# Layer 2 attention of a four-layer kernel: two-pass scores, and row maxima carried by DMA one tile at a time

## The chip, the cores and the metric

The kernel runs on one core of a Trainium2 chip. The metric is device time in microseconds, the median of the runs. Engines: PE (matmul; PEld is its weight load), DVE (vector), ACT (scalar), POOL, and SP, which here only issues DMAs.

## What is computed

Four layers in turn on x, 4 sequences of 1024 tokens, 256 wide; after each, x = layernorm(x + layer(x)). The change lies in the second, a causal softmax attention with 8 heads of 64, whose values come from routed experts:

```python
q = (x @ w_q).reshape(b, n, HEADS, DIM_HEAD).transpose(0, 2, 1, 3)
k = (x @ w_k).reshape(b, n, HEADS, DIM_HEAD).transpose(0, 2, 1, 3)
...
values = jnp.einsum('bhne,ehdk,bnd->bhnk', gm, value_experts, x)
sim = jnp.einsum('bhid,bhjd->bhij', q * SCALE, k)
causal_mask = jnp.triu(jnp.ones((n, n), dtype=bool), 1)
sim = jnp.where(causal_mask, jnp.finfo(sim.dtype).min, sim)
attn = jax.nn.softmax(sim, axis=-1)
out = jnp.einsum('bhij,bhjk->bhik', attn, values)
```

## The kernel before

`layer2` (L429) loops over the four sequences. Each passes three stages, blocks in which every engine has its own written-out order and which end in a barrier: `gates_and_values` (L470: routing weights, values), `attention` (L590) and `output_experts`. Semaphores alone tie the engines together; nothing is scheduled by a planner.

**Precision.** A fast matmul takes operands rounded to float32r. So q and k are split into a rounded part (hi) and a rest (lo). For head h, slot h % 4 of `kst` holds k hi on one half of the 128 partitions and k lo on the other; `qst` holds q hi on both; `qlo` q lo on both. The scores of a key tile (128 keys by up to 512 queries, a "unit"; 12 units per head) are three matmuls in one PSUM bank: kst x qst (L662), kst x qlo (L663), and -max of each query, as `negones` x `shift` (L666), where `shift` is the identity times the maxima. A unit on the diagonal gets a mask matmul too (L665). Three banks (0 to 2) rotate.

**Maxima.** Before that, `maxima` (L648, L650) computes the scores of a query tile by all its keys with hi parts only, 1024 keys wide down to 128, into banks 3 and 4; DVE takes their row maxima (L769) and POOL makes `shift` (L785). For the first five tiles of a head, PE waits until the maximum before has been read; later the two banks alternate. In head 0, banks 5 and 6 are used too.

**The rest.** ACT takes exp of each unit (L703). `weighted` (L674, fp32) sums probabilities times values over key tiles in banks 5 and 6; its first one waits until DVE has copied the head before to `oT` (L759) and ACT its denominators (`den`, L725), which SP sends to `dens` (L622). `project` (L635) makes q and k of two heads in four parts (k, k, q, q, each 512 tokens), through bank 7; ACT copies the hi parts (L715, L718), DVE subtracts for the lo parts (L749, L753).

**The order.** Steps 0 to 9, each of eight k: scores of head step-2, maxima of head step-1, and in steps 0, 2, 4, 6 the projection of the next two heads at k = 0, 1, 2, 4. The last weighted sum of a head comes before the next head's first scores:

```python
for step in range(H0 + 2):
    h1, h2 = step - 1, step - 2
    for k in range(NT):
        if h2 >= 0:
            scores(h2, k)
        ...
    if h2 >= 0:
        weighted(h2, NT - 1)
```

Below, "head n's stretch" is the time from its first score matmul to the next head's, whatever else runs in it.

Of the kernel before, what the change touches and what calls it, by code (L numbers as in the profile page):

```python
# [29 lines left out]
P = 128  # L30
# [391 lines left out]
ATTN2 = ("qk_mm qk_hi qk_parts max_mm max_read shift_ready score_mm exp_ready pv_mm o_read den_read "  # L422
# [6 lines left out]
def layer2(nc, ctx, m, I, src, dst):  # L429
# [39 lines left out]

    def gates_and_values(own):  # L470
# [14 lines left out]
        with nc.Block() as block:  # L485
# [7 lines left out]
            def _(pe):  # L493
# [7 lines left out]
                for n, (h, t) in enumerate(order):  # L501
# [10 lines left out]
                    last.then_inc(s.value_mm, 1)  # L512

# [76 lines left out]
    def attention(own, b):  # L590
# [3 lines left out]
        kst, qst, qlo = (sb(n, [P, RK, T], F32R) for n in ("kst", "qst", "qlo"))  # L594
        shift = sb("shift", [P, 2, T], F32R)
        prob = sb("prob", [P, 2, T])
        mx = sb("mx", [P, H0, NT])
# [5 lines left out]
        parts = [(kind, n) for kind in "kq" for n in range(NH)]  # L603
        part_at = {0: 0, 1: 1, 2: 2, 4: 3}
# [10 lines left out]
        with nc.Block() as block:  # L615
            @block.sync
            def _(sp):
                fetch_load(sp, m, s, src[(b + 1) % SEQS])
                sp.dma_start(oe[:, :, :], I["oe2"][:, 0]).then_inc(s.oe_in, 16)
                for h in range(H0):  # L620
                    sp.wait_ge(s.den_read, h + 1)
                    sp.dma_start(dens[h:h + 1, :], den[den_row(h), h % 2, :]).then_inc((s.even_den_out, s.odd_den_out)[h % 2], 16)  # L622
                sp.wait_ge(s.even_den_out, 16 * (H0 // 2))
# [4 lines left out]
            def _(pe):  # L628
# [10 lines left out]
                def maxima(h, k):  # L639
                    t = NT - 1 - k  # L640
                    if k == 0:
                        pe.wait_ge(s.qk_parts, 4 * (h // 2 + 1))
# [10 lines left out]
                def scores(h, k):  # L653
                    for n, (kk, lo, hi) in enumerate(units, U * h):
                        if kk != k:
                            continue
                        if n % U == 0:
                            pe.wait_ge(s.shift_ready, NT * (h + 1))
                        if n >= 3:
                            pe.wait_ge(s.exp_ready, n - 2)  # L660
                        out, keys = bank(m.ps, n % 3, 0, hi - lo), kst[:, h % RK, k * P:(k + 1) * P]
# [16 lines left out]
                for step in range(H0 + 2):  # L678
                    h1, h2 = step - 1, step - 2
                    for k in range(NT):  # L680
                        if h2 >= 0:
                            scores(h2, k)
                        if step % 2 == 0 and step < H0 and k in part_at:
                            project(step // 2, part_at[k])
                        if 0 <= h1 < H0 and k < NT - 1:
                            maxima(h1, k)
                        if h2 >= 0 and k >= 1:
                            weighted(h2, k - 1)
                        if 0 <= h1 < H0 and k == NT - 2:
                            maxima(h1, NT - 1)  # L690
                    if h2 >= 0:
                        weighted(h2, NT - 1)

            @block.scalar
            def _(act):
# [10 lines left out]
                def hi_parts(c, j):  # L706
# [5 lines left out]
                    for odd in (0, 1):  # L712
                        got, slot = bank(m.ps, proj_bank(c, j), 0, HALF, half(odd)), (2 * c + odd) % RK
                        if kind == "k":
                            last = act.copy(kst[half(odd), slot, cols], got)  # L715
# [11 lines left out]
                for step in range(H0 + 2):  # L727
                    h2 = step - 2
                    for k in range(NT):
                        if h2 >= 0:  # L730
                            exps(h2, k)
                        if k == 0 and h2 >= 1:
                            den_out(h2 - 1)
                        if k == 3 and step == H0 + 1:
                            fetch_sd(act, m, s)
                        if step % 2 == 0 and step < H0 and k in part_at:
# [1162 lines left out]
```

## Time and profile before

| | us |
|---|---|
| median of 3 runs | 3823.37 (3819.16 to 3826.95) |
| the profiled execution | 3819.95 |
| its span, first to last instruction | 3818.2 |
| PE busy | 3343.3 (88%) |
| DVE, ACT, POOL busy | 2084.4, 1465.2, 830.3 |
| mean granted TensorE clock | 0.930 of full |

The profile comes from one execution, so sums are made against its own 3819.95. An engine's busy share is a mean over stages with different limits; of a busy PE one must know that matmuls overlap, so that what one matmul costs is the distance from its start to the next start. In idle columns the name behind the arrow is what ended the wait.

### The profile page before, as it was taken

How to read it: one execution, taken by the hardware profiler on the slowest of the kernel's cores; microseconds unless marked ns; L12 is line 12 of the kernel's file. 1: busy time of each engine (PE TensorE's matmuls, PEld its weight loads, DVE VectorE, ACT ScalarE, POOL GpSimd, SP SyncE). 2: the span in 40 equal slices, each digit the busy share in tenths (PEclk: the TensorE clock that was granted, in tenths of full speed). 3: DMA queues.
4: the chain of work that ended last, by engine and by line, in shares of the span. 5: the costliest groups of instructions: out<-in, count | busy, mean ns of one | idle time of the engine just before them, and what ended most of it. 6: DMA issues, size and time to landing. Idle time of an engine off the chain costs nothing. (4 is left out here: it accounts for less than half of the span.)

```text
span 3818.2 us, 51310 instructions
## 1 busy us (share of the span) xinstructions
PE 3343.3 (88%) x18610; PEld 2417.7 (63%) x18610; DVE 2084.4 (55%) x3495; ACT 1465.2 (38%) x2638; POOL 830.3 (22%) x908
## 2 busy tenths in 40 slices
PE   6896898988989989888998698998989698989898
PEld 4555655975568755786558555546465476767676
DVE  4346844677445954569446474756657433333333
ACT  2321144412444134431344355563645433434343
POOL 1111411743137422454216300101010000000000
PEclk9897999988999999989999899998998899999999
DMA  5111100110011100111002101000000310000000
GB/s 180 44 44 56 44 1 24 52 40 28 1 45 42 35 22 1 68 32 44 1 1 75 56 2 24 1 13 13 2 23 2 117 52 12 12 12 12 12 12 12
DMA packets 139735, 121.01 MB, mean 32 GB/s; under 512 B 79696, under 2 KB 121936, under 8 KB 136016
## 3 DMA queue, kind: packets, MB, share of 16 engines
q1 hardware_dynamic: 139472, 117.45, 10.1%
q8 instruction: 172, 2.82, 0.3%
q14 instruction: 91, 0.75, 0.1%
HBM read 100.23 MB, written 28.31 MB: 34 GB/s over the span
## 5 line engine op out<-in xcount | busy, mean ns | idle before, releaser
L1378 ACT ACTIVATE l3b_prob<-sums 128x512 f32<-128x512 f32 (+3 forms) x768 | 333.0, 494 | 205.1 <-PE sums L1311 166.6
L1628 PE MATMUL sums<-l4a_uhi,l_h 128*128 128x512 f32 x1024 | 405.8, 396 | 0.0
L1628 PE MATMUL sums<-l4a_ulo,l_h 128*128 128x512 f32 x1024 | 403.8, 394 | 0.0
L842 POOL TENSOR_TENSOR l2c_rlo<-l2c_routed,l2c_rhi 128x512 fp32r<-128x512 f32 x256 | 348.4, 1374 | 214.0 <-ACT l2c_rhi L868 177.9
L769 DVE TENSOR_REDUCE l2b_mx<-sums 128x1 f32<-128x1024 f32 (+7 forms) x256 | 192.0, 757 | 318.9 <-PE sums L650 318.2
L703 ACT ACTIVATE l2b_prob<-sums 128x512 f32<-128x512 f32 (+3 forms) x384 | 186.6, 491 | 397.7 <-PE sums L666 393.2
L1673 DVE TENSOR_TENSOR l4a_ulo<-l4a_made,l4a_uhi 128x512 fp32r<-128x512 f32 x192 | 132.1, 688 | 375.1 <-ACT l4a_uhi L1641 374.2
L222 POOL COPY sb_x<-sb_nx 128x2048 f32<-128x2048 f32 x12 | 23.0, 1914 | 1322.6 <-POOLq L1742 571.1
L952 PE MATMUL sums<-l2c_ohi,l2c_rhi 128*128 128x256 f32 x1024 | 294.4, 287 | 12.8 <-POOL l2c_rlo L842 12.1
L674 PE MATMUL sums<-l2b_prob,l_vx 128*128 128x512 f32 (+3 forms) x768 | 301.0, 506 | 3.3 <-ACT l2b_den L725 1.9
L1306 PE MATMUL sums<-l_qst,l_kst 64*128 64x512 f32 (+3 forms) x768 | 279.3, 427 | 16.4 <-DMA l_qst<-l3b_peak 6.7
L952 PE MATMUL sums<-l2c_ohi,l2c_rlo 128*128 128x256 f32 x1024 | 291.9, 285 | 0.0
L952 PE MATMUL sums<-l2c_olo,l2c_rhi 128*128 128x256 f32 x1024 | 291.8, 285 | 0.0
L785 POOL TENSOR_SCALAR l2b_shift<-sb_ident,l2b_mx 128x128 fp32r<-128x128 f32 x256 | 154.2, 605 | 603.7 <-DVE l2b_mx L769 491.0
L1289 PE MATMUL sums<-l_kst,l_qst 64*128 64x512 f32 (+3 forms) x768 | 244.1, 443 | 18.9 <-DVE l3b_low L1390 10.4
L905 DVE TENSOR_TENSOR l2c_routed<-l_oT,sums 128x512 f32<-128x512 f32 x256 | 171.6, 682 | 149.3 <-PE sums L942 148.2
L868 ACT CAST l2c_rhi<-l2c_routed 128x512 fp32r<-128x512 f32 x256 | 158.2, 621 | 238.2 <-DVE l2c_routed L905 236.8
L1306 PEld LDWEIGHTS sums<-l_qst,l_kst 64*128 64x128 f32 x768 | 140.8, 195 | 153.9 <-ACT l3b_prob L1378 133.6
L203 PE MATMUL sums<-sb_ident,sb_nx 128*128 128x128 f32 x256 | 61.0, 421 | 194.4 <-issue 93.0
L1628 PEld LDWEIGHTS sums<-l4a_uhi,l_h 128*128 128x128 f32 x1024 | 192.4, 188 | 47.5
L1628 PEld LDWEIGHTS sums<-l4a_ulo,l_h 128*128 128x128 f32 x1024 | 192.4, 188 | 45.6
L662 PE MATMUL sums<-l2b_qst,l2b_kst 128*128 128x512 f32 (+3 forms) x384 | 207.5, 540 | 7.9 <-POOL l2b_shift L785 7.9
(247 smaller groups left out, 8141.3 us busy)
## 6 DMA issues: line engine op xcount, KB each, us to landing
l_ve<-ve SPq DMA_DIRECT2D x34, 512.0 KB, 4.0
l_oe<-oe SPq DMA_DIRECT2D x16, 1024.0 KB, 6.2
sb_nx<-sums SPq DMA_DIRECT2D x15, 1024.0 KB, 5.5
l2c_word<-weights_copy SPq DMA_DIRECT2D x32, 352.0 KB, 4.0
weights_copy<-h SPq DMA_DIRECT2D x2, 4096.0 KB, 25.9
l_qst<-l3b_peak SPq DMA_DIRECT2D x512, 0.5 KB, 2.0
l_h<-weights_copy SPq DMA_DIRECT2D x2, 4096.0 KB, 23.9
sb_nx<-tokens SPq DMA_DIRECT2D x5, 1024.0 KB, 5.7
```

What stands on the lines that cost most here:

```text
L662: pe.matmul(out, keys, qst[:, h % RK, lo:hi], start=True, stop=False)
L674: last = pe.matmul(bank(m.ps, PV, lo, hi), vx[:, k, h, :], prob[:, k % 2, lo:hi], start=(k == 0), stop=True, skip_group_check=True)
L703: act.activation(prob[:, k % 2, lo:hi], bank(m.ps, n % 3, 0, hi - lo), ACT.Exp, scale=SCALE0).then_inc(s.exp_ready, 1)
L769: dve.reduce_max(mx[:, h1, t:t + 1], bank(m.ps, max_bank(h1, k), 0, (t + 1) * P), AX_X).then_inc(s.max_read, 1)
L842: pool.tensor_tensor(rlo[:, i % RT, :], routed[:, i % RT, :], rhi[:, i % RT, :].bitcast(F32), ALU.subtract).then_inc(s.routed_lo, 1)
L868: act.copy(rhi[:, i % RT, :], routed[:, i % RT, :]).then_inc(s.routed_hi, 1)
L905: dve.tensor_tensor(routed[:, i % RT, :], oT[:, c, n * HALF:(n + 1) * HALF], bank(m.ps, 4 + i % 4), ALU.mult).then_inc(s.routed, 1)
L952: last = pe.matmul(m.ps[:, t * D:(t + 1) * D], r[:, k % RT, cols], w[:, c % 2, e, :], start=(c == e == 0 and t % 2 == 0 and r is rhi and w ...
L1289: last = pe.matmul(bank(m.ps, at, 0, hi - lo), qst[rows(a), p, t * P:(t + 1) * P], kst[rows(a), p, lo:hi], start=True, stop=True)
L1306: last = pe.matmul(bank(m.ps, part % SCORE, 0, hi - lo), kst[rows(a), p, k * P:(k + 1) * P], qst[rows(a), p, lo:hi], start=True, stop=True)
L1378: act.activation(prob[:, i % RB, j, a, 0:hi - lo], bank(m.ps, part % SCORE, 0, hi - lo), ACT.Exp, scale=SCALE1).then_inc(s.exp_ready, 1)
L1628: run(lambda out, a, x, first, last: pe.matmul(out, a, x, start=first, stop=last))
```

## The change

- **Two passes.** `qlo`, `shift` and L663 go. New tiles `krow` and `qrow` hold, per slot, 65 rows: k hi (64 rows) over a row of -1, and q lo over a row of maxima. A unit is now kst x qst and krow x qrow, which gives k hi x q lo - max. (k lo x q lo was in the sum before and is not now.) ACT copies k hi twice; DVE makes q lo once instead of twice.
- **Maxima.** POOL's multiplication goes (it only sets the row of -1 once). `mx` is float32r, and SP sends each tile's 128 maxima, one element per partition, into row 64 of `qrow`. SP waits for each maximum in turn; the denominators of the head before are sent after the eighth.
- **Ticks.** The three loops now run over one counter x. Maxima of head h are at ticks 8 + 8h onwards, scores at 18 + 8h (two ticks later than the end of the maxima), and the weighted sum of a key tile comes in the tick after its scores, also across heads. The parts are k, k, q (second half of the tokens), q (first half), at ticks 0 to 3 and then every second tick from the first scores of heads 0, 2 and 4.
- **Warm-up matmuls** with no use of their result: 8 after the values, 8 after the first projections, 1 after each maxima of head 0.

```diff
+    def warm(pe, at, times):
+        for _ in range(times):
+            pe.matmul(bank(m.ps, at), sel[:, 0, :], sel[:, 0:HALF // P, :], start=True, stop=True)
...
                     last.then_inc(s.value_mm, 1)
+                warm(pe, 7, 8)
...
+        parts = [("k", 0), ("k", 1), ("q", 1), ("q", 0)]
+        WAIT = 2
+        APART = 2
+        ticks = NT * (H0 + 2) + WAIT + 1
+        scored_in = lambda x: divmod(x - 2 * NT - WAIT, NT)
+        peaked_in = lambda x: divmod(x - NT, NT)
...
+        def project_in(x):
+            if x < 4:
+                return 0, x
+            c, ahead = divmod(x - WAIT, 2 * NT)
+            if 1 <= c < H0 // 2 and ahead in range(0, 4 * APART, APART):
+                return c, ahead // APART
...
                 for h in range(H0):
+                    if h >= 2:
+                        sp.wait_ge(carried[h % 2], carried_to(h - 2))
+                    if h >= RK:
+                        sp.wait_ge(s.score_mm, U * (h - RK + 1))
+                    for k in range(NT):
+                        t = NT - 1 - k
+                        sp.wait_ge(s.max_read, NT * h + k + 1)
+                        sp.dma_start(qrow[DH0:ROWS, h % RK, t * P:(t + 1) * P].bitcast(F32),
+                                     mx[:, h, t:t + 1].bitcast(F32)).then_inc(carried[h % 2], 16)
+                    if h >= 1:
+                        den_row_out(h - 1)
+                den_row_out(H0 - 1)
...
-                        pe.matmul(out, keys, qst[:, h % RK, lo:hi], start=True, stop=False)
-                        pe.matmul(out, keys, qlo[:, h % RK, lo:hi], start=False, stop=False)
+                        pe.matmul(out, kst[:, h % RK, at], qst[:, h % RK, lo:hi], start=True, stop=False)
...
-                        pe.matmul(out, m.negones[:, :], shift[:, h % 2, lo:hi], start=False, stop=True).then_inc(s.score_mm, 1)
+                        pe.matmul(out, krow[0:ROWS, h % RK, at], qrow[0:ROWS, h % RK, lo:hi], start=False,
+                                  stop=True).then_inc(s.score_mm, 1)
...
+                for x in range(ticks):
+                    h2, k2 = scored_in(x)
+                    h1, k1 = peaked_in(x)
+                    if has(h2):
+                        scores(h2, k2)
+                    if project_in(x):
+                        project(*project_in(x))
+                        if x == 3:
+                            warm(pe, 6, 8)
+                    if has(h1):
+                        maxima(h1, k1)
+                        if h1 == 0:
+                            warm(pe, PROJ, 1)
+                    h2, k2 = scored_in(x - 1)
+                    if has(h2):
+                        weighted(h2, k2)
```

**PE, from head 0's last tiles into head 1.** L674 / L713 are weighted sums, L662 / L701 the first score pass, L648 / L685 maxima, L650 / L687 and L665 / L703 masks. Before:

```order
L674 MATMUL sums<-l2b_prob,l_vx 128x256 [waits l2_attn_exp_ready]
L674 MATMUL sums<-l2b_prob,l_vx 128x128 [waits l2_attn_exp_ready]
L662 MATMUL sums<-l2b_qst,l2b_kst 128x512 [waits l2_attn_exp_ready,l2_attn_shift_ready]
L663 MATMUL sums<-l2b_qlo,l2b_kst 128x512
L665 MATMUL sums<-sb_mask_kq,sb_ident 128x128
L666 MATMUL sums<-l2b_shift,sb_negones 128x512
L662 MATMUL sums<-l2b_qst,l2b_kst 128x512 [waits l2_attn_exp_ready]
L663 MATMUL sums<-l2b_qlo,l2b_kst 128x512
L666 MATMUL sums<-l2b_shift,sb_negones 128x512
L648 MATMUL sums<-l2b_kst,l2b_qst 128x512 [waits l2_attn_max_read,l2_attn_qk_parts]
```

Twelve more rows follow before the first weighted sum of head 1. In the changed kernel:

```order
L687 MATMUL sums<-sb_mask_qk,sb_ident 128x128
L713 MATMUL sums<-l2b_prob,l_vx 128x128 [waits l2_attn_exp_ready]
L701 MATMUL sums<-l2b_qst,l2b_kst 128x384 [waits l2_attn_exp_ready]
L703 MATMUL sums<-sb_mask_kq,sb_ident 128x128
L704 MATMUL sums<-l2b_qrow,l2b_krow 128x384
L701 MATMUL sums<-l2b_qst,l2b_kst 128x512 [waits l2_attn_exp_ready]
L704 MATMUL sums<-l2b_qrow,l2b_krow 128x512
L685 MATMUL sums<-l2b_kst,l2b_qst 128x512 [waits l2_attn_max_read]
L685 MATMUL sums<-l2b_kst,l2b_qst 128x128
L687 MATMUL sums<-sb_mask_qk,sb_ident 128x128
L713 MATMUL sums<-l2b_prob,l_vx 128x512 [waits l2_attn_den_read,l2_attn_o_read,l2_attn_exp_ready]
```

Between the last weighted sum of head 0 (128x128) and the first of head 1 (128x512) stood 20 matmuls with a whole first tile's scores and maxima; now 8 stand there.

**DVE, start of head 2's stretch.** L769 / L806 are the maxima, L749 / L789 the k lo parts, L759 / L798 the copy of a finished head. Before:

```order
L769 TENSOR_REDUCE l2b_mx<-sums 128x1 [waits l2_attn_max_mm] x8
L759 COPY l_oT<-sums 64x1024 [waits l2_attn_pv_mm]
L769 TENSOR_REDUCE l2b_mx<-sums 128x1 [waits l2_attn_max_mm]
L749 TENSOR_TENSOR l2b_kst<-sums,l2b_kst 64x512 [waits l2_attn_qk_hi]
L749 TENSOR_TENSOR l2b_kst<-sums,l2b_kst 64x512
L769 TENSOR_REDUCE l2b_mx<-sums 128x1 [waits l2_attn_max_mm]
```

In the changed kernel:

```order
L806 TENSOR_REDUCE l2b_mx<-sums 128x1 [waits l2_attn_max_mm] x8
L789 TENSOR_TENSOR l2b_kst<-sums,l2b_kst 64x512 [waits l2_attn_qk_hi]
L789 TENSOR_TENSOR l2b_kst<-sums,l2b_kst 64x512
L798 COPY l_oT<-sums 64x1024 [waits l2_attn_pv_mm]
L806 TENSOR_REDUCE l2b_mx<-sums 128x1 [waits l2_attn_max_mm] x2
```

The copy of the finished head has moved behind a maximum and the two subtractions, which wait for ACT.

**ACT, a k part.** Before:

```order
L715 CAST l2b_kst<-sums 64x512 [waits l2_attn_qk_mm]
L715 CAST l2b_kst<-sums 64x512
L715 CAST l2b_kst<-sums 64x512 [waits l2_attn_qk_mm]
L715 CAST l2b_kst<-sums 64x512
L718 CAST l2b_qst<-sums 64x512 [waits l2_attn_qk_mm]
```

In the changed kernel:

```order
L755 CAST l2b_kst<-sums 64x512 [waits l2_attn_qk_mm]
L756 CAST l2b_krow<-sums 64x512
L755 CAST l2b_kst<-sums 64x512
L756 CAST l2b_krow<-sums 64x512
L755 CAST l2b_kst<-sums 64x512 [waits l2_attn_qk_mm]
```

Two more copies stand in each k part.

## Rows read from the trace of the kernel before

**Rows 1.** The page, part 1: busy us, share of span, instructions.
```profile
PE 3343.3 (88%) x18610; PEld 2417.7 (63%) x18610; DVE 2084.4 (55%) x3495; ACT 1465.2 (38%) x2638; POOL 830.3 (22%) x908
```

**Rows 2.** Busy time by stretches: second attention stage, and the sum of four.
```profile
core 0: us, PE busy (x) PEld busy (x) DVE busy (x) ACT busy (x) POOL busy (x), PEclk, DMA share, GB/s
...
900.20:1107.50 207.30, 189.51 (x768) 113.21 (x768) 96.65 (x149) 84.07 (x155) 38.54 (x64) 0.94 0.03 11
...
sum 825.20, PE 754.36 PEld 451.04 DVE 386.38 ACT 335.98 POOL 154.18; mean PE 188.59 PEld 112.76 DVE 96.60 ACT 84.00 POOL 38.54
```

**Rows 3.** The same view, heads 1, 4, 5 and 7 of the second stage.
```profile
955.90:976.20 20.30, 20.30 (x89) 12.84 (x89) 7.08 (x9) 6.90 (x13) 4.84 (x8) 0.92 0.00 1
...
1023.90:1052.90 29.00, 26.22 (x107) 15.08 (x106) 15.63 (x22) 13.74 (x25) 4.79 (x8) 1.00 0.00 1
...
1052.90:1071.70 18.80, 18.80 (x89) 12.03 (x89) 7.11 (x9) 6.79 (x13) 4.85 (x8) 1.00 0.01 1
...
1090.40:1107.50 17.10, 16.15 (x70) 10.11 (x69) 8.27 (x31) 9.62 (x17) 0.00 (x0) 1.00 0.01 2
```

**Rows 4.** Timeline (start, us) of PE, then ACT: second and third stage's start.
```profile
900.30 5.98 PE L635 MATMUL sums<-l_xT,l_wk 128*128 128x512 f32 x8 [4.57 <-PEq L485]
...
916.10 1.22 PE L648 MATMUL sums<-l2b_kst,l2b_qst 128*128 128x512 f32 x2 [6.38 <-DVE l2b_qlo L753]
...
925.18 0.80 PE L662 MATMUL sums<-l2b_qst,l2b_kst 128*128 128x512 f32 x1 [1.39 <-POOL l2b_shift L785]
...
1350.54 3.67 PE L635 MATMUL sums<-l_xT,l_wk 128*128 128x512 f32 x8 [2.97 <-PEq L485]
...
1373.12 0.80 PE L662 MATMUL sums<-l2b_qst,l2b_kst 128*128 128x512 f32 x1 [1.40 <-POOL l2b_shift L785]
...
1352.53 1.17 ACT L715 CAST l2b_kst<-sums 64x512 fp32r<-64x512 f32 x2 [25.57 <-PE sums L635]
...
1355.97 4.73 ACT L718 CAST l2b_qst<-sums 64x512 fp32r<-64x512 f32 x8 [0.55 <-PE sums L635]
```

**Rows 5.** Timeline of PE in head 5 of the second stage.
```profile
1053.24 0.39 PE L663 MATMUL sums<-l2b_qlo,l2b_kst 128*128 128x512 f32 x1
...
1053.47 0.23 PE L665 MATMUL sums<-sb_mask_kq,sb_ident 128*128 128x128 bf16 x1
```

**Rows 6.** Groups by line and shape: busy us, mean ns | idle before.
```profile
L662 PE MATMUL sums<-l2b_qst,l2b_kst 128*128 128x512 f32 x192 | 96.7, 503 | 7.9 <-POOL l2b_shift L785 7.9
...
L1306 PE MATMUL sums<-l_qst,l_kst 64*128 64x512 f32 x384 | 156.2, 478 | 11.5 <-DMA l_qst<-l3b_peak 6.7 <-ACT l3b_prob L1378 2.2
...
L769 DVE TENSOR_REDUCE l2b_mx<-sums 128x1 f32<-128x1024 f32 x32 | 39.2, 1225 | 78.7 <-PE sums L650 78.7
...
L759 DVE COPY l_oT<-sums 64x1024 f32<-64x1024 f32 x32 | 39.1, 1222 | 34.1 <-PE sums L674 34.1
...
L749 DVE TENSOR_TENSOR l2b_kst<-sums,l2b_kst 64x512 fp32r<-64x512 f32 x64 | 44.1, 689 | 23.2 <-ACT l2b_kst L715 22.0
...
L715 ACT CAST l2b_kst<-sums 64x512 fp32r<-64x512 f32 x64 | 37.2, 581 | 157.2 <-PE sums L635 156.8
...
L769 DVE TENSOR_REDUCE l2b_mx<-sums 128x1 f32<-128x768 f32 x32 | 30.6, 957 | 68.3 <-PE sums L650 68.3
```

**Rows 7.** Timeline of PE, second k part of head 4's stretch.
```profile
1030.69 1.98 PE L635 MATMUL sums<-l_xT,l_wk 128*128 128x512 f32 x4 [1.34 <-DVE l2b_kst L749]
```

**Rows 8.** DMA issue of the page (KB, us to landing); tile l3b_peak.
```profile
sb_nx<-sums SPq DMA_DIRECT2D x15, 1024.0 KB, 5.5
...
L1277 SPq DMA_DIRECT2D l_qst<-l3b_peak x512: 468/601/1578, 2212.7 to 2995.9; - x171
...
DMA to landing us min/median/max: 1.9/2.0/3.4
```

**Rows 9.** Timeline of PE in layer 4, after two gaps.
```profile
3157.52 0.62 PE L1628 MATMUL sums<-l4a_xhi,l_w 128*128 128x512 f32 x1 [2.85 <-DVE l4a_made L1713]
...
3350.74 0.50 PE L1628 MATMUL sums<-l4a_xhi,l_w 128*128 128x512 f32 x1 [2.85 <-DVE l4a_made L1713]
```

More of the change, by code:

```diff
@@ L592, in attention @@
         RK = 4
-        kst, qst, qlo = (sb(n, [P, RK, T], F32R) for n in ("kst", "qst", "qlo"))
-        shift = sb("shift", [P, 2, T], F32R)
+        kst, qst = sb("kst", [P, RK, T], F32R), sb("qst", [P, RK, T], F32R)
+        krow, qrow = sb("krow", [P, RK, T], F32R), sb("qrow", [P, RK, T], F32R)
+        ROWS = DH0 + 1
         prob = sb("prob", [P, 2, T])
-        mx = sb("mx", [P, H0, NT])
+        mx = sb("mx", [P, H0, NT], F32R)
         den = sb("den", [P, 2, T])
@@ L602, in attention @@
         through = lambda k: sum(kk <= k for kk, _lo, _hi in units)
-        parts = [(kind, n) for kind in "kq" for n in range(NH)]
-        part_at = {0: 0, 1: 1, 2: 2, 4: 3}
+        parts = [("k", 0), ("k", 1), ("q", 1), ("q", 0)]
[4 more added lines that the diff above has]
+        peaked_in = lambda x: divmod(x - NT, NT)
+        has = lambda h: 0 <= h < H0
+        carried = (s.even_carried, s.odd_carried)
+        carried_to = lambda h: 16 * NT * (h // 2 + 1)
+        def project_in(x):
[4 more added lines that the diff above has]
+                return c, ahead // APART
         MAX, PV, PROJ = 3, 5, 7
@@ L641, in maxima @@
                     if k == 0:
[L642 removed]
+                        pe.wait_ge(s.qk_parts, 4 * (h // 2) + 2)
+                        pe.wait_ge(s.qk_hi, 4 * (h // 2) + 3)
+                    if k == NT // 2:
+                        pe.wait_ge(s.qk_hi, 4 * (h // 2) + 4)
                     if h and k <= NT // 2:
@@ L676, in weighted @@
                     last.then_inc(s.pv_mm, 1)
[L678 to L692, printed above, removed]
+                for x in range(ticks):
[14 more added lines that the diff above has]
+                        weighted(h2, k2)
             @block.scalar
@@ L714, in hi_parts @@
                         if kind == "k":
-                            last = act.copy(kst[half(odd), slot, cols], got)
+                            act.copy(kst[half(odd), slot, cols], got)
+                            last = act.copy(krow[half(0), slot, cols], got)
                         else:
@@ L725, in den_out @@
                     act.copy(den[den_row(h), h % 2, :], bank(m.ps, PV, 0, T, den_row(h))).then_inc(s.den_read, 1)
[L727 to L736, printed above, removed]
-                            hi_parts(step // 2, part_at[k])
+                for x in range(ticks):
+                    h2, k2 = scored_in(x)
+                    if has(h2):
+                        exps(h2, k2)
+                    if project_in(x):
+                        hi_parts(*project_in(x))
+                    if k2 == 0 and 1 <= h2 < H0:
+                        den_out(h2 - 1)
+                    if (h2, k2) == (H0 - 1, 3):
+                        fetch_sd(act, m, s)
                 den_out(H0 - 1)
@@ L751, in lo_parts @@
                         else:
-                            for to in (0, 1):
-                                last = dve.tensor_tensor(qlo[half(to), slot, cols], got, qst[half(odd), slot, cols].bitcast(F32),
-                                                         ALU.subtract)
+                            last = dve.tensor_tensor(qrow[half(0), slot, cols], got, qst[half(odd), slot, cols].bitcast(F32),
+                                                     ALU.subtract)
                     last.then_inc(s.qk_parts, 1)
@@ L778, in _ @@
                 clear(pool, s1)
-                for h in range(H0):
-                    if h >= 2:
-                        pool.wait_ge(s.score_mm, U * (h - 1))
-                    for k in range(NT):
-                        t = NT - 1 - k
-                        pool.wait_ge(s.max_read, NT * h + k + 1)
-                        pool.tensor_scalar(shift[:, h % 2, t * P:(t + 1) * P], m.ident[:, :], mx[:, h, t:t + 1], None,
-                                           ALU.mult).then_inc(s.shift_ready, 1)
+                pool.memset(krow[DH0:ROWS, :, :].bitcast(F32), -1.0).then_inc(s.row_ready, 1)
     def output_experts(own, b):
```

33 lines of the change are left out of this document (18 added, 15 removed).

## Prediction

> **What bounds the kernel now.** I read the page's busy shares first: PE is busy 88% of the span, DVE 55%, ACT 38%, POOL 22% [rows 1]. PE is the engine to look at, but a share says nothing of where, so next came the busy time by stretches. The four attention stages of layer 2, from the first projection to the last weighted sum, take 825.2 us together, 22% of the span; the second takes 207.3 us [rows 2]. The change touches nothing else but the tail of the stage before. Cut by heads (from one head's first score matmul to the next head's), a stage has three kinds of stretch [rows 3]. A plain head (at 1052.9) takes 18.8 us, all of it PE busy, in 89 matmuls. A head beside which the q and k of later heads are projected (at 1023.9) takes 29.0, PE busy 26.22. The last, without maxima, takes 17.1. The head at 955.9 is a plain one that took 20.3 at a mean clock of 0.92: 1.5 us more, for a short time at 1.2 instead of 2.4 GHz. So in the body PE sets the pace, and a matmul less is time less, unless a wait takes its place.
>
> The start of a stage is otherwise. Project, copy out (ACT), subtract (DVE), maxima, shift (POOL), first score: 24.9 us in the second sequence (900.30 to 925.18), 22.6 in the third (1350.54 to 1373.12) [rows 4]. PE sits idle 6.38 us of it until the last l2b_qlo is there. The body is then 825.2 - 3 x 24.9 - 22.6 = 727.9 us, 182.0 per sequence (the first and fourth are taken as like the second).
>
> **The change, part by part.**
>
> *1. One score pass less.* L663 goes: 12 matmuls per head. What one costs is not its duration (overlapped) but the time from its start to the next start: 0.23 us for 512 columns (1053.24 to 1053.47) [rows 5]. By width, read the same way from the 89 matmuls of that head (0.18 for 384 columns, 0.125 for 256, 0.115 for 128), 6 x 0.23 + 2 x 0.18 + 2 x 0.125 + 2 x 0.115 = 2.2 us per head, 8 heads, 17.7 per sequence. The matmul with 65 rows (krow, qrow) stands where the one with 128 rows (negones, shift) stood. No row has 65; between the 64-row and 128-row ones the mean durations are 478 and 503 ns [rows 6], so I take no change, and 0.025 x 12 x 8 = 2.4 us per sequence either way for the range.
>
> *2. Maxima two ticks ahead of the scores.* The order shows 11 maxima on DVE ahead of the first k part where there were 9. Two tiles (1024 and 896 columns, 0.49 + 0.56 us start to start) thus run on PE before the first score: -1.05.
>
> *3. Projections.* Their PE work stays: 26.22 - 18.8 is 7.4, with a switch more about 7.5 per pair of heads, 22.5 for the three in the body. What changes is the chain behind each part. ACT makes 4 copies of 0.58 us for a k part (2 before); DVE makes 2 subtractions of 0.69 us for a q part (4 before) [rows 6]. A part needs 4 x 0.58 + 2 x 0.69 + latencies = 3.85 us from its last matmul until the single bank is free. Before, the second k part found the bank taken for 1.34 us [rows 7]. Now the parts are two ticks apart. PE has 4.4 us of work between the first three, but only 3.1 before the fourth: 0.75 idle. The fourth's subtractions stand on DVE ahead of the 896-wide maximum, and the next maxima wait for its bank: 0.9.
>
> *4. New waits at a head's end.* The last weighted sum of a head now comes after the next head's first scores, while the first weighted sum of the next head stays at its second tile and still waits for l_oT and l2b_den. DVE at that place first does the 768-wide maximum (0.96 us), then the 1.22 us copy [rows 6]: from the start of the mask matmul of those maxima 0.27 (its 0.23 [rows 5] and 0.04 to reach DVE) + 0.96 + 0.04 + 1.22 + 0.05 back to PE = 2.54 us. PE has 0.06 + 0.21 (weighted) + 1.02 (scores) + 0.40 (maxima) = 1.69 to do, start to start from the same 89 matmuls, without L663. It idles 0.85, at six boundaries, and 0.55 at the last, where there is no maximum. Before, PE had some 4 us in that place. At the starts of heads 2 and 4 the first k part's subtractions stand ahead of that copy, and they wait for ACT's four copies: 2.5 more each. The 896-wide maxima wait for the 1024-wide maximum (1.225 us [rows 6]) with one pair of banks: 0.27 + 1.225 + 0.05 = 1.55 against 0.06 + 0.64 (weighted) + 0.32 (scores) = 1.02, so 0.53, at six heads.
>
> *5. The maxima's way.* POOL's shift (0.6 us) goes; a DMA on SP's queue takes each tile of maxima into qrow. Layer 3 does the same: 0.6 us to issue, 2.0 us to land, 3.4 at worst [rows 8]. Queued on SP behind these waits is the row of denominators of the head before; after it is free SP has 8 x 0.6 = 4.8 us to issue in seven ticks. The last tile's DMA lands 3.2 us after its maxima, PE gets there after 4.0: hidden by 0.8 us of two ticks' work. Where ticks carry no maxima (last boundary) 0.5 shows. If that cover were gone, all 2.0 us would show at each head. POOL's memset of one partition (4096 elements) runs beside 22 us of start: nothing. The Trainium skill speaks against this step ("DMA: Bandwidth & Descriptors", Rules for kernel authors): coalesce small transfers, since under 64 KB one pays mostly overhead. By that rule the 256 transfers of 0.5 KB are overhead, and one exposed landing per head would give 32 x 2.0 = 64 us, so 3842 instead of 3778 (an estimate, from the landing of rows 8).
>
> Body: the 182.0 of now is 7 x 18.75 + 17.1 + 3 x 10.3 = 179.2 at full clock, and the rest the clock (part 7). Anew: 7 x 18.75 + 17.1 = 148.35; less 17.7 and 1.05 = 129.6; plus 22.5 = 152.1; plus the waits 6 x 0.53 + 6 x 0.85 + 0.55 + 3 x 1.65 + 2 x 2.5 + 0.5 = 19.3; in all 171.4.
>
> *6. The start.* Eight matmuls (0.23 us each) now follow the values and cut PE's idle time before the projections from 4.57 us to 2.7. That idle time seems to decide the clock: after 4.57 us the eight k rows took 5.98 us, after 2.97 (third sequence) 3.67 [rows 4]; in layer 4 a gap of 2.85 us was followed once by a matmul of 0.62 us (1.2 GHz) and once by one of 0.50 (2.4 GHz) [rows 9]. I take the fast case, and 1.9 us per sequence for the range. ACT then starts 2.0 us in (1350.54 to 1352.53); 16 copies are 2 x 4.73 = 9.5 [rows 4]; DVE's last pair 1.4; the first maximum at 12.9. Eight maxima of head 0 take 6.6 as before, the DMA 2.5 with its queue: first score at 22.0, against 24.9 and 22.6. PE's warm-up matmuls there run beside DVE and cost nothing. Four starts: 97.3 becomes 88.0.
>
> *7. The clock.* All four bodies now begin at 1.2 GHz (0.80 us for the matmul at 925.18 [rows 4], 0.50 in the mean [rows 6]). With less idle time ahead I count half of that cost, 0.8, and 0.7 for the two long stalls of part 4: 1.5.
>
> Sum: 4 x (171.4 + 1.5) + 88.0 = 779.6 against 825.2: **-45.6 us**. The profiled execution took 3820.0 us (span 3818.2); that gives 3774.4. The median of the three runs is 3.4 above it, so **3778 us**.
>
> **Rivals.**
> - A, *the waits are less than I add up*. The 19.3 + 1.5 us per sequence of parts 3, 4 and 7 are differences of small numbers. For it: removed matmuls can only shorten PE's side; the idle times I read in the body (29.00 - 26.22 = 2.8 per projecting head, 1.0 in the last [rows 3]) sit only there. Against: DVE's two long operations are measured, and the order is fixed. With half of them: 3778 - 42 = 3736; below that only if nearly all vanish (3695).
> - B, *the clock*. The change puts short idle times of 0.5 to 3.4 us into every head where there were none. The head at 955.9 shows the price when PE falls to 1.2 GHz for a short stretch: 20.3 - 18.8 = 1.5 us. If each of 32 heads pays it: 48, which takes back the gain: 3778 + 48 = 3826. Against: the head at 1023.9 has an idle time of 1.34 us and a clock of 1.00 [rows 3, 7]. The Trainium skill knows this mechanism ("TensorE: Matmul & The Clock Gate", A second HAM failure mode): frequent short idle times between matmul groups on cycling PSUM banks make the clock oscillate. The trace bears it out in the head at 955.9, not in the one at 1023.9 with the same kind of gap.
> - C, *the carried maxima come late* (slower). Place: the first score matmul of each head, which waits for all eight DMAs. If a landing takes L instead of 2.0 us, 28 heads lose L - 2.8 and the four first ones L - 2.0: 32 L - 86.4. It ends slower than before from L = 4.1 on. At 5.5 us, what the 1 MB load on the same queue takes [rows 8]: 3778 + 90 = 3868. For it: eight DMAs of 128 single elements in a row, one queue, the denominators in between. Against: layer 3's 512 of them, worst 3.4.
>
> **How the numbers follow.** Forecast, with waits between half and 1.4 times mine (3736 to 3778 + 33 = 3811, which also holds the 2.4 and 1.9 us per sequence of parts 1 and 6): 0.77. A, below 3736: 0.08. B: 0.09. C: 0.06. The range is 3736 to 3812; 0.2 or a little more lies outside. Less than 0.2% (7.6 us) is about what a measurement of this kernel can't tell from no change: faster means below 3815.7. Forecast and A are faster, 0.85, less 0.02 for cases close to it; B lies at 3826, within, and its spread gives 0.06 to same and 0.03 to slower; C is slower. With the 0.02: faster 0.83, same 0.08, slower 0.09.
>
> **What would show it.** Right: the four attention stages at about 195 us each; a plain head at 17.9 us with PE idle once behind the 1024-wide maximum and once before a head's first weighted sum, named as a wait for l_oT; no idle 6.38 before the first maxima; l2b_mx landing in 2 us. Wrong: score matmuls waiting for a DMA of l2b_mx over 1 us in most heads (C); plain heads without idle but over 17 us at a clock under 0.95 (B); plain heads at 16.5 us (A).

## The result, and the profile after

The changed kernel takes 3781.17 us in the median of 5 runs (3777.82 to 3796.23), the kernel before 3823.37 (3819.10 to 3835.22): a ratio of 0.9897, 95% interval 0.9872 to 0.9921. The forecast was 3778, with a range of 3736 to 3812. The profiled run took 3777.82 us (span 3776.1). From the page:

```profile
PE 3284.2 (87%) x18322; PEld 2357.3 (62%) x18322; DVE 2038.9 (54%) x3431; ACT 1494.3 (40%) x2702; POOL 688.9 (18%) x656
...
L713 PE MATMUL sums<-l2b_prob,l_vx 128*128 128x512 f32 (+3 forms) x768 | 309.2, 513 | 38.6 <-DVE l_oT L798 23.8
```

PE is busy 59 us less than in [rows 1], but the span is only 42 us shorter: waits have come in. The weighted sums now idle 38.6 us. The second attention stage with the sum of the four, and then heads 0 to 4 and 6 of the second stage, show where (length, PE, PEld, DVE, ACT, POOL, clock, DMA share, GB/s, as in [rows 2, 3]):

```profile
892.04:1086.24 194.20, 173.38 (x688) 97.14 (x688) 85.28 (x132) 91.17 (x170) 3.50 (x1) 0.97 0.06 12
...
sum 778.85, PE 694.61 PEld 389.66 DVE 341.03 ACT 365.00 POOL 14.02; mean PE 173.65 PEld 97.42 DVE 85.26 ACT 91.25 POOL 3.50
```

```profile
916.68:941.25 24.57, 23.50 (x92) 12.73 (x92) 10.50 (x15) 14.76 (x28) 0.00 (x0) 1.00 0.03 1
941.25:959.98 18.73, 16.98 (x78) 9.86 (x77) 8.25 (x12) 6.67 (x13) 0.00 (x0) 1.00 0.04 1
959.98:987.79 27.81, 23.81 (x95) 13.03 (x93) 11.64 (x16) 15.65 (x29) 0.00 (x0) 1.00 0.03 1
987.79:1006.52 18.73, 16.99 (x79) 9.87 (x77) 8.26 (x12) 6.68 (x13) 0.00 (x0) 1.00 0.04 1
1006.52:1035.75 29.23, 25.23 (x94) 13.59 (x93) 11.63 (x16) 15.65 (x29) 0.00 (x0) 0.94 0.02 1
...
1054.47:1070.56 16.09, 15.41 (x73) 9.23 (x71) 5.97 (x8) 6.43 (x13) 0.00 (x0) 1.00 0.05 2
```

The four stages take 778.85 us; measured the same way they took 824.66 before. That is the whole gain, 45.8 us; the rest of the program became 3.7 us longer. (A stage is the stretch from the first projection to the last weighted sum.) The surprise is in the heads: heads 1, 3 and 5 take 18.73 us, as the plain heads did with a whole score pass more (18.8 [rows 3]). Head 0 gives most (30.7 to 24.6 here, 26.1 in the other stages), then head 6 (18.7 to 16.1), head 7 and head 2 (over 1 us each). Head 1 took 20.3 in three of the four stages before, at a granted clock of 0.92, and gives that clock back. Not every stretch is at full clock now either: head 4 has 0.94 in three stages and 0.89 in the first (29.2 to 29.3 and 30.8 us, where head 2 takes 27.8 at 1.00), and head 0 has 0.93 to 0.94 in three stages (26.1 to 26.2 us, against 24.6 at 1.00). Timeline of PE, where it stood idle in heads 2 to 4:

```profile
968.18 1.96 PE L713 MATMUL sums<-l2b_prob,l_vx 128*128 128x512 f32 x4 [2.98 <-DVE l_oT L798]
...
986.90 0.68 PE L685 MATMUL sums<-l2b_kst,l2b_qst 128*128 128x512 f32 x2 [0.37 <-DVE l2b_mx L806]
990.04 0.61 PE L685 MATMUL sums<-l2b_kst,l2b_qst 128*128 128x512 f32 x2 [0.84 <-DVE l2b_mx L806]
992.95 1.95 PE L713 MATMUL sums<-l2b_prob,l_vx 128*128 128x512 f32 x4 [0.54 <-ACT l2b_prob L743]
...
1014.72 3.36 PE L713 MATMUL sums<-l2b_prob,l_vx 128*128 128x512 f32 x4 [2.98 <-DVE l_oT L798]
```

The row at 992.95 names ACT's probabilities, but what let that weighted sum go was DVE's copy of the finished head:

```profile
991.64 1.21 DVE L798 COPY l_oT<-sums 64x1024 f32<-64x1024 f32 x1
```

It ends at 992.85, 0.10 us before the weighted sum starts. In 24 of the 28 places where a head's first weighted sum follows a finished head, it starts 0.10 us after that copy's end, whatever name the row has; in the other four (the last head of a stage) ACT's copy of the denominators comes last.

Head 3 holds the waits of 990.04 and 992.95 and one of 0.37 at 1005.64 for its 896-wide maxima. Counted start to start (each is some 0.15 us more than the idle time shown) they come to about 2.2 us, as much as the pass that was removed. Which of these waits is a matter of order, and what the pass itself is worth, only runs can tell.

### The profile page after: what moved, and what is told of

Same layout as the page of the kernel before. It is cut to its first block and busy times, and to the rows that moved or that the text cites. A ratio compares the mean times of both kernels' runs of the same rounds, so it can differ in the third digit from the quotient of the medians.

```text
span 3776.1 us, 50816 instructions
## 1 busy us (share of the span) xinstructions
PE 3284.2 (87%) x18322; PEld 2357.3 (62%) x18322; DVE 2038.9 (54%) x3431; ACT 1494.3 (40%) x2702; POOL 688.9 (18%) x656
## 5 line engine op out<-in xcount | busy, mean ns | idle before, releaser
L806 DVE TENSOR_REDUCE l2b_mx<-sums 128x1 fp32r<-128x1024 f32 (+7 forms) x256 | 193.0, 757 | 310.8 <-PE sums L687 309.0
L713 PE MATMUL sums<-l2b_prob,l_vx 128*128 128x512 f32 (+3 forms) x768 | 309.2, 513 | 38.6 <-DVE l_oT L798 23.8
L1321 PE MATMUL sums<-l_kst,l_qst 64*128 64x512 f32 (+3 forms) x768 | 237.9, 432 | 20.3 <-DVE l3b_low L1422 10.3
L514 PE MATMUL sums<-l2a_vhi,l2a_xhi 128*128 128x512 f32 x512 | 204.5, 399 | 16.3 <-DVE l2a_vm L564 12.8
L701 PE MATMUL sums<-l2b_qst,l2b_kst 128*128 128x512 f32 (+3 forms) x384 | 215.2, 560 | 0.0
```

The source lines that it names most:

```text
L514: last = pe.matmul(bank(m.ps, n % RING), x[:, c, t * P:(t + 1) * P], v[:, h % 2, c, :], start=(c == 0 and x is xhi and v is vhi), stop=(c ...
L701: pe.matmul(out, kst[:, h % RK, at], qst[:, h % RK, lo:hi], start=True, stop=False)
L713: last = pe.matmul(bank(m.ps, PV, lo, hi), vx[:, k, h, :], prob[:, k % 2, lo:hi], start=(k == 0), stop=True, skip_group_check=True)
L806: dve.reduce_max(mx[:, h1, t:t + 1], bank(m.ps, max_bank(h1, k1), 0, (t + 1) * P), AX_X).then_inc(s.max_read, 1)
L1321: last = pe.matmul(bank(m.ps, at, 0, hi - lo), qst[rows(a), p, t * P:(t + 1) * P], kst[rows(a), p, lo:hi], start=True, stop=True)
```

## The experiments

Each was timed in 4 to 8 runs beside 11 or 13 of the kernel before, which took 3822.5, 3822.92 and 3823.94 us in the three sessions. "Stages" is the sum of the four attention stages in the profiled run: before 824.7, the change 778.9. It tells more than the total, because the rest of the program moves by itself (last section).

### The removed product alone

```diff
-                        pe.matmul(out, keys, qlo[:, h % RK, lo:hi], start=False, stop=False)
```

> The kernel before with one thing taken out: the third score product (queries' low part times keys' high part), so the scores lack one small term. Nothing of the reordering of maxima, copies and layer 3's blocks is in it. Before this run the changed kernel took 3781 us against 3823. Theory W (the product is worth its full 2.2 us a head as long as the order leaves no wait in its place; in the changed kernel the maxima carried tile by tile and the copy of the output give some of it back as waits): 32 heads x 2.2 = 70 us less, minus whatever the maxima of the old order hold up: 3753 to 3763 us, so faster than the changed kernel. Rival P (DVE's maxima and copies, not PE, pace a head once the product is gone, in either order): about 42 us less, 3778 to 3785 us.

3791.03 us (3789.35 to 3804.84), ratio 0.9927 (0.9908 to 0.9946); 32 less than the kernel before; stages 788.0, 36.7 less. Theory W expected 60 to 70 and is out by half; P's 3778 to 3785 isn't met either. The product alone gives four fifths of the stages' gain (36.7 of 45.8 us), and all the rest of the change together (order, carried maxima, filler matmuls) 9.1 more. Order and carried maxima were not run apart from each other. Heads 2, 3 and 5 of the second stage, from the stretches of this run:

```profile
962.77:991.13 28.36, 24.54 (x93) 12.90 (x92) 15.73 (x22) 13.51 (x25) 4.79 (x8) 1.00 0.00 1
991.13:1009.65 18.52, 18.19 (x76) 10.83 (x76) 7.02 (x9) 6.79 (x13) 4.83 (x8) 0.92 0.00 1
1038.00:1055.12 17.12, 16.80 (x77) 9.98 (x77) 7.01 (x9) 6.68 (x13) 4.84 (x8) 1.00 0.00 0
```

A plain head loses 1.65 us. A projecting head loses 0.6 only: PE's work there fell by 1.7 (26.22 [rows 3] to 24.54), but PE had idled 2.8 us, for the parts' chain of copies and subtractions and for one maximum, and now idles 3.8. In head 3 the clock is 0.92 and takes the gain back; in the kernel before it was head 1 that paid this. Head by head in the second stage (us, from one head's first score to the next's):

```
head                      0      1      2      3      4      5      6      7
before                  30.7   20.3   29.0   18.8   29.0   18.8   18.7   17.0
product removed         30.0   17.1   28.4   18.5   28.4   17.1   17.1   15.6
the change              24.6   18.7   27.8   18.7   29.2   18.7   16.1   15.7
copy ahead of split     27.4   18.7   25.6   18.7   25.6   18.7   16.1   15.7
tick reordered          26.2   17.7   25.3   17.8   25.3   17.8   16.2   15.6
```

Against the product removed alone, the change gains in head 0 (5.4 us here, about 4 in the other stages), head 6 (1.0) and head 2 (0.6). It loses 1.6 us in heads 1 and 5, and 0.8 in head 4, where the clock is 0.94.

### Shorter maxima, with three products and with two

The same edit, in the kernel before and in the one with the product removed:

```diff
-                            dve.reduce_max(mx[:, h1, t:t + 1], bank(m.ps, max_bank(h1, k), 0, (t + 1) * P), AX_X).then_inc(s.max_read, 1)
+                            dve.reduce_max(mx[:, h1, t:t + 1], bank(m.ps, max_bank(h1, k), 0, min((t + 1) * P, HALF)), AX_X).then_inc(s.max_read, 1)
```

> The kernel before, all three products, with the same shorter maxima (first 512 keys of the four widest tiles; the shift of the softmax is another number). It shows what the maxima's length cost before the change. Theory W (with three products nearly every wait for a maximum is covered): idle of L648 behind DVE l2b_mx is 4.24 us a stage now, so up to 17 us less, 3806 to 3819 us. Rival P (DVE paces both orders): 30 us less or more, 3793 or below.

> The kernel before without its third score product and with the same shorter maxima. With the kernels without the product (3791 us) and with the shorter maxima alone this makes the square: does the product become worth its 70 us (32 x 2.2) once the maxima hold nothing up? Theory W: yes, the missing 35 us were waits for maxima; 3755 to 3766 us. Rival P2 (the product itself is worth no more than about 1.3 us a head, whatever DVE does): the difference to the kernel with shorter maxima alone stays 31 to 40 us, so 3770 us or more.

3807.71 us (0.9958, 0.9943 to 0.9973) and 3772.02 us (0.9865, 0.9848 to 0.9881); stages 805.7 and 768.1. The square of the stages: with full maxima the product is worth 824.7 - 788.0 = 36.7, with short ones 805.7 - 768.1 = 37.6. The first run is as theory W had it, the second as P2: the missing half was not a wait for maxima. By heads with short maxima: plain 18.56 to 16.60, both without any idle time of PE and at full clock, so 1.96 where I had 2.2; projecting 28.43 to 27.55, 0.9; the last 17.0 to 15.6, 1.35. In plain heads the product is worth nearly its time; where a chain of copies sets the pace, it isn't.

### A product put back in the new order

```diff
+                        pe.matmul(out, krow[0:ROWS, h % RK, at], qrow[0:ROWS, h % RK, lo:hi], start=False, stop=False)
                         pe.matmul(out, krow[0:ROWS, h % RK, at], qrow[0:ROWS, h % RK, lo:hi], start=False,
```

> The changed kernel with each maxima product of queries and keys issued twice (the output then holds that term twice). 32 heads x 10 products of about 0.22 us = 71 us of TensorE. Theory W (part of the pass taken out had been turned into waits, so part of a pass put back fills them): 30 to 55 us more, 3811 to 3836 us, and the waits of L685 and L713 shrink. Rival P2 (the waits are separate from the pass): 65 to 75 us more, 3846 to 3856 us.

What is issued twice is the second score product, the one that carries the maxima (krow x qrow, 12 matmuls per head), not the products that the maxima are taken from. 3836.13 us (1.0040, 1.0026 to 1.0054): 55 more than the change, at W's upper edge and far from P2; stages 836.4, 57.6 more (14.4 per stage, against 9.2 in the order of before). The waits shrink as W had it, those of L713 from 38.6 to 27.7 us and those of L685 from 37.8 to 29.5. Heads 1, 3 and 5 take 19.94, only 1.2 more, and PE idles 0.86 us in them instead of 1.74: over a third of the pass fills waits there. Head 6, which has few, takes 1.8 more. Heads 0 and 2 take some 3 us more, which is more than the product: their clock fell too (head 2 from 1.00 to 0.94 in all four stages). With three products the new order is slower than the old one (836.4 against 824.7).

### The copy of a head's output, ahead of the split

DVE's part; on ACT `den_out` likewise moves ahead of `hi_parts`:

```diff
-                    if project_in(x):
-                        lo_parts(*project_in(x))
                     if k2 == 0 and 1 <= h2 < H0:
                         head_out(h2 - 1)
+                    if project_in(x):
+                        lo_parts(*project_in(x))
```

> The changed kernel with the copy of a head's output sum and of its denominators issued ahead of the split of the queries' parts on DVE and ACT, instead of behind it. Theory W (at heads 2 and 4 the first weighted product waits 2.98 us for that copy, of which the split ahead of it is about half): 8 places x 1.5 = 12 us less, about 3769 us, if the first maxima product of the next head, which needs the split, does not become late by as much. Rival (that product takes the wait over): 3781 us, within 3.

3753.24 us (3749.54 to 3761.61), ratio 0.9823 (0.9804 to 0.9843): 28 less, over twice what W expected; stages 753.9, 24.9 less. It is in heads 2 (27.8 to 25.6) and 4 (29.2 to 25.6), which give 25.3 in all; the plain heads stay. The groups of PE within the stages, here:

```profile
L713 PE MATMUL sums<-l2b_prob,l_vx 128*128 128x512 f32 (+3 forms) x768 | 303.1, 504 | 20.2 <-ACT l2b_prob L743 12.2 <-issue 5.4 <-ACT l2b_den L766 2.6
```

The 23.8 us of waits for l_oT of the page above (8 of 2.98) have become 5.4 (8 of 0.68) named "issue"; it is still the same wait, for these weighted sums too start 0.10 us after the copy's end. I had counted 1.5 per place, about the two subtractions that stood ahead of the copy (1.39). But they wait 0.91 us for ACT's copies first, and that is saved as well: 2.24 at each of the 8 places, 18 us. The other 7 us are clock, which is 1.00 in head 4 now.

### A second copy in that place

```diff
+                    dve.tensor_copy(spare[vcol(h), :], bank(m.ps, PV, 0, T, vcol(h)))
```

> The changed kernel with a second, useless copy of the same size (1.22 us in the trace) on DVE ahead of each head's copy of its output sum. Theory W (the first weighted product of a head waits for that copy, so what is put ahead of it is paid at each of the 7 head boundaries): 28 x 1.22 = 34 us more, 3812 to 3818 us, and the idle time of L713 behind DVE l_oT grows from some 6 to some 14 us a stage. Rival A (the wait has slack behind it, and PE waits for the maxima next in any case): 0 to 10 us more.

3840.30 us (1.0044, 1.0030 to 1.0059), 59 more, and stages 831.6, 52.7 more, where W said 34. Rival A is out. Plain heads at full clock take 19.87, 1.14 more for 1.22 us of copy, so the copy is on the path there too, as its end 0.10 us before the weighted sum in the change said and the name in the row at 992.95 did not. The surplus is mostly clock: head 3, for one, takes 21.5 at 0.92 in three of the four stages and 19.87 at 1.00 in the last. The timeline of this run, at the first weighted sums of heads 1, 2 and 3 of the second stage:

```profile
957.24 1.96 PE L714 MATMUL sums<-l2b_prob,l_vx 128*128 128x512 f32 x4 [1.67 <-issue]
...
980.15 3.48 PE L714 MATMUL sums<-l2b_prob,l_vx 128*128 128x512 f32 x4 [4.12 <-DVE l_oT L800]
...
1007.76 3.64 PE L714 MATMUL sums<-l2b_prob,l_vx 128*128 128x512 f32 x4 [1.67 <-issue]
```

Four matmuls take 1.96 us at 2.4 GHz (granted clock 1.00) and 3.5 mostly at 1.2 GHz (0.54 in these 3.5 us); head 2 takes 30.7 instead of 27.8, 1.1 of it the copy.

### Shorter maxima in the change

The edit is that of the square above, in line 806.

> The changed kernel with the maxima of the four widest query tiles taken over the first 512 keys alone (the softmax is then shifted by another number; nothing else changes). DVE's longest operation falls from 1.225 to about 0.69 us. Theory W (TensorE waits for the 1024-wide and 896-wide maxima with the one pair of banks, about 1.5 us per plain head, and the copy of the output comes that much earlier): plain heads 18.7 -> 17.2 to 17.6, 1.0 us or more per head, 30 to 45 us less, 3736 to 3751 us, and the idle time of L685 behind DVE l2b_mx, 9 to 10 us a stage now, falls below 4. Rival (the wait moves on to the next consumer, the weighted product, which waits for ACT's probabilities by the profile's naming): 3765 us or more.

3755.91 us (0.9827, 0.9811 to 0.9842), 25 less; stages 755.8, 23.0 less. It lies between both. Plain heads fall to 18.05 (0.7, not 1.1 to 1.5) and the idle time of L685 to 6.5 us a stage, not below 4. So the maxima's length costs about half of what I gave it. Only 8 of the 23 us are in the plain heads: the starts, in which eight maxima stand one behind the other, give 7.0, and head 0 gives 8.0, in part because it is at full clock in all four stages. The wait behind the fourth part, whose subtractions stand ahead of the maximum on DVE, stays: 0.84 us before, 0.97 here.

### One tick less between maxima and scores

```diff
-        WAIT = 2
+        WAIT = 1
```

> The changed kernel with one tick less between a head's maxima and its scores, so that the row of maxima (2 us from issue to landing, ten small transfers at 1.0 us each to issue) has less to hide behind. Theory W (the carried maxima are covered now with little to spare): scores wait for the transfer, 14 to 25 us more, 3795 to 3806 us. Rival (cover is ample): within 3 of 3781 us, or up to 10 less from the shorter start.

3797.99 us (0.9933, 0.9916 to 0.9950), 17 more, as W; stages 803.7, 24.9 more. All 32 first score matmuls start 0.09 us after the last transfer of their maxima has landed. PE stands idle before them for 0.3 us in most heads, for 0.9 in the last of a stage and 1.3 to 1.8 in the first, 18.9 us in all (mostly named "issue" in the row below), where it stood idle for none. Not all of the 24.9 is the transfer's: one maximum of head 1 is back in the body, head 2 is at a clock of 0.94 in all four stages, and six of the twelve plain heads are at 0.91 or 0.92. In the change the last transfer lands 1.3 to 2.6 us before the scores of most heads, 0.2 to 0.9 before those of a stage's first head, and 0.09 before those of its last, in all four stages: there the two ticks are just enough. So rival C of the prediction was closer in its mechanism than the change shows.

```profile
L701 PE MATMUL sums<-l2b_qst,l2b_kst 128*128 128x512 f32 (+3 forms) x384 | 218.8, 570 | 18.9 <-issue 16.9 <-DVE l2b_qrow L792 2.0
```

### The filler matmuls: none, or more

```diff
-        for _ in range(times):
+        for _ in range(0):
```

> The changed kernel without its filler matmuls at the start of each sequence, which only keep TensorE busy. Theory W (they stand in idle time and hold the granted clock up for the projections behind them): 1 to 2.5 us more per sequence, 3785 to 3791 us, and the key rows' projection takes 5.4 us or more in all four sequences. Rival (they stand in the way of work that is ready): 3781 us or less.

3792.87 us (0.9935, 0.9915 to 0.9955), 12 more; stages 796.3, 17.4 more. W's direction, but not its place: the key rows take 5.37, 3.67, 5.19 and 6.75 us, over 5.4 in one stage only, and the starts give 4.0 of the 17.4. The other 13.4 are in the bodies (from a stage's first score matmul on), 174.5 us in the mean against 171.1: PE idles as long there as in the change, but head 2 is at a clock of 0.94 or 0.89 in all four stages instead of 1.00. Why filler matmuls at a stage's start change the clock 40 us and more behind them stays open.

This run also answers what the new order and the carried maxima are worth without filler matmuls: nothing here. It took 3792.87 us and its stages 796.3; the kernel with only the product removed, without filler matmuls too, took 3791.03 and 788.0.

```diff
-                warm(pe, 7, 8)
+                warm(pe, 7, 18)
```

> The changed kernel with 18 instead of 8 filler matmuls at the start of each sequence, which reach over the 2.79 us in which TensorE idles ahead of the projections. Theory W (that gap costs the clock in two of the four sequences: 5.4 and 6.7 us for the key rows instead of 3.67): 4 to 8 us less, 3773 to 3777 us. Rival (the first score is held by the maxima, which are held by DVE, so the clock of the key rows is hidden): within 2 of 3781 us.

3778.80 us (0.9891, 0.9875 to 0.9907): by the total not to be told from the change, so neither W nor its rival is decided by it. In the stages it shows: 776.4, 2.5 less; the gap before the key rows is 0.3 to 0.6 us instead of 2.79, and all four starts take 22.5 to 22.8 us.

### Another order within a tick

On PE the weighted sums of the tick before move ahead of the maxima; on DVE the copy of the output stands first, then the maximum, then the split (ACT as above):

```diff
+                    h2, k2 = scored_in(x - 1)
+                    if has(h2):
+                        weighted(h2, k2)
                     if has(h1):
                         maxima(h1, k1)
...
-                    h2, k2 = scored_in(x - 1)
-                    if has(h2):
-                        weighted(h2, k2)
```

> The changed kernel with another order of work in a tick. TensorE: scores, projection, weighted products, maxima products (the weighted products stood behind the maxima). DVE: copy of the output, then the maxima's reductions, then the split of the queries. Theory W (the two waits of a head, of the maxima for their bank and of the weighted products for the output's copy, are waits of order and not of work): 10 to 30 us less, 3751 to 3771 us. Rival (each order only moves the wait to the next consumer, here the weighted products wait for the probabilities of the scores just ahead of them): 3781 to 3800 us.

**3731.90 us** (3728.77 to 3734.38), ratio 0.9763 (0.9750 to 0.9776): 49 less than the change, with the same instructions, and below both kernels. Of the 49, the stages hold 37.3:

```profile
sum 741.56, PE 688.22 PEld 397.04 DVE 341.03 ACT 365.41 POOL 14.02; mean PE 172.06 PEld 99.26 DVE 85.26 ACT 91.35 POOL 3.50
```

12.4 of it comes on top of what moving the copy alone gave, mostly from the plain heads, 18.73 to 17.77: the weighted sums' wait is gone, in the groups of PE:

```profile
L713 PE MATMUL sums<-l2b_prob,l_vx 128*128 128x512 f32 (+3 forms) x768 | 293.0, 490 | 5.6 <-ACT l2b_prob L743 3.1 <-ACT l2b_den L766 2.6
L685 PE MATMUL sums<-l2b_kst,l2b_qst 128*128 128x512 f32 (+3 forms) x384 | 183.5, 532 | 36.5 <-DVE l2b_mx L808 36.1
```

The 38.6 us of L713 are 5.6 now, and L685's idle time stayed as it was (37.8 in the change). In the last head of each stage the scores now wait 0.55 us for the transfer of their maxima. The profiled run is 11.2 us shorter than the change's outside the stages, where this edit changes nothing (last section).

> The kernel of the reordered tick (weighted products ahead of the maxima product, copy of the output first on DVE; 3732 us) with 18 instead of 8 filler matmuls at the start of each sequence. Theory W (two of its four starts take 24.1 to 24.4 us and two 22.5, the difference being the key rows at half clock; the longer filler gave that alone in the changed kernel, 2.5 us in the stages): 2 to 5 us less, 3727 to 3730 us. Rival (what the starts gain is lost to the clock elsewhere): within 2 of 3732 us.

The edit is the sum of the last two. 3742.14 us (3726.80 to 3749.42), ratio 0.9787 (0.9769 to 0.9805): inconclusive. The stages are the shortest of all, 731.0, and its fastest run the fastest of all, but the median is 10 above the kernel without it, with runs 23 us apart. By the total the edit isn't shown to help.

## Why the prediction held, by its steps

- **The sum.** 4 x (171.4 + 1.5) + 88.0 = 779.6 was forecast for the stages, 778.85 measured. That it comes within a microsecond is luck, for errors of opposite sign cancel. The starts took 94.3 us (88.0 forecast), 6.3 more. At full clock the eight heads of a stage come to 168.2 (24.6 + 3 x 18.7 + 2 x 27.8 + 16.1 + 15.7), not 171.4, so 13 less in four stages. The clock then cost 3.0 us per sequence, not 1.5, so 6 more. The mechanism held: the pass goes, and waits come in its place.
- **Part 1, the pass.** 2.2 us per head is too high: 1.96 in a plain head without waits (the square), less where others set the pace. The matmul with 65 rows costs no more than the one it replaced (399 ns in the mean, 403 before), as assumed.
- **Part 3.** The 0.9 behind the fourth part is there, 0.84 idle, but in the plain head behind it and not in the projecting head, where the sum has it. This is why the check "a plain head at 17.9" failed at 18.73. A projecting head with a copy to wait for is 29.6 by my terms (18.75 - 2.2 + 7.5 + 0.53 + 0.75 + 0.9 + 0.85 + 2.5) and took 27.8; without the 0.9 they give 28.7. The 0.75 before the fourth part was 0.65.
- **Part 4, the wait for the copy.** At heads 2 and 4 2.98 idle, 3.35 forecast; in the plain heads 0.54 for 0.85, under ACT's name and not l_oT's, though the copy's end released it. In the kernel with only the product removed, the copy ended 1.8 to 7.3 us before it was needed: the wait came with the new order. The 896-wide maxima: 0.37 idle, about 0.53 start to start, as forecast.
- **Part 5, the DMAs.** They land in 1.9 us in the median. One issue takes 0.6 us where SP has fallen behind (946.22, 946.79, 947.43 and 948.08 in the change), as forecast; otherwise SP waits for the maxima themselves. (The 1.0 us each in the expectation for the shorter wait holds SP's waiting.) At the last head, where 0.5 was forecast, the scores start 0.09 behind the landing and PE shows no idle time. Small transfers are what the Trainium skill advises against ("DMA: Bandwidth & Descriptors", Rules for kernel authors), and the prediction's estimate for one exposed landing per head was 3842. Here, with two ticks of cover, PE idles for none of the 256; with one tick it idles 18.9 us.
- **Parts 2 and 6, the start.** This is the step that failed. I forecast 22.0 each and got 24.46, 24.64, 22.61 and 22.62. The first two maxima of head 1 were taken out of the body (part 2) and not put into the start, where they now run before the first score, the second of them after a wait for the first (1.32 us at 916.13): some 0.6 us in each start. And the gap of 2.79 gave half clock in two of four sequences, not in none: the key rows took 5.37 and 6.68 us there, 3.67 in the others.
- **Part 7 and rival B.** Seven of eight heads of the second stage are at a clock of 1.00 with one to three waits each, so B did not come as a price in every head. But seven of the 32 heads pay it, head 4 in every stage and head 0 in three, 12 us together; part 7 had 6. **Rival A** did not come unaided. With half of the waits of parts 3, 4 and 7 the stages would take 738; the reordered tick, which takes waits out, came to 741.6.

## What to carry to other kernels

When a unit of work goes from the bounding engine, look in each kind of stretch for what comes next there: one score pass per head was worth 1.65 us where PE was full and 0.6 where a chain of copies set the pace. After such a change read the order on the helper engines again: what the bounding engine waits for belongs ahead of what is needed two ticks later, and two moves of this kind took 37.3 us from the stages, where the change as a whole had taken 45.8. Where a change brings several things, run each alone: here the removed product gave 36.7, and what was left of the gain went when the filler matmuls did. The name of a wait is a hint; compare its end with the ends of all that it could have waited for. And compare stages, not totals, when the effect is under half a per cent.

## What the runs showed of the hardware

The clock does not follow from the length of a gap alone. In the change, the same idle time of 2.98 us was followed by four matmuls in 1.96 us at 2.4 GHz (968.18, granted clock 1.00) and, 46.5 us later, in 3.36 us mostly at 1.2 GHz (1014.72, granted clock 0.58), and so in all four stages: head 2 at 27.8, head 4 at 29.2 to 30.8. In the run with the second copy, 1.67 us of idle time was followed by both (957.24 at 1.00, 1007.76 at 0.53).

Code that no experiment touches did not take the same time. From the end of the last attention stage to the end of the program, with the same 10402 matmuls, the change took 1816.1 us; the reordered tick and the kernel with the second copy show (columns as above):

```profile
1920.86:3727.60 1806.74, 1575.30 (x10402) 1139.75 (x10402) 913.16 (x1654) 827.23 (x1542) 154.41 (x104) 0.93 0.09 24
```

```profile
2014.05:3841.40 1827.35, 1596.46 (x10402) 1156.34 (x10402) 914.96 (x1655) 826.18 (x1542) 154.12 (x104) 0.92 0.09 24
```

They are 20.6 us apart, with DVE and ACT busy within 2 us of each other and PE 21 us more in the longer one. The granted clock differs with it, 0.933 against 0.921. What sets it there stays open. It is why totals here say less than stages.
